# Layer 2's attention in a four-layer transformer kernel: the order of TensorE's work within a step

## The reference

```python
x = layernorm(...)                                   # [4, 256, 512]
q = rms_norm(x @ Wq + bq, gq)                        # [4, 256, 32 * 128]
k = rms_norm(x @ Wk + bk, gk)
v = x @ Wv + bv
# 32 heads of 128
p = softmax(q_h @ k_h.T / sqrt(128))                 # [4, 32, 256, 256]
o = p @ v_h
x = x + concat(o) @ Wo + bo
```

## Time and profile before

| | |
|---|---|
| median of 3 runs | 2597.18 us (2591.51 to 2602.34) |
| the profiled execution's own time | 2593.06 us |
| its span in the trace | 2591.2 us |
| granted TensorE clock, mean | 0.98 |
| busy: PE, DVE, ACT, POOL | 95%, 64%, 40%, 36% of the span |
| layer 2's attention stage | about 1488 to 2130 us of the span |

### The profile page before, as it was taken

How to read it: one execution, slowest core, us unless ns; L and a number is a source line. 1 busy time by engine, 2 the same in 40 slices (tenths; PEclk the granted TensorE clock), 3 DMA queues, 4 the chain that set the end, 5 groups by cost and what they waited for, 6 DMA issues and landing times. The chain is left out here.

```text
span 2591.2 us, 40725 instructions
## 1 busy us (share of the span) xinstructions
PE 2451.2 (95%) x14448; PEld 1958.6 (76%) x14448; DVE 1666.4 (64%) x2390; ACT 1030.5 (40%) x2030; POOL 941.3 (36%) x581
## 2 busy tenths in 40 slices
PE   5989999999969989999999989999999999999799
PEld 4767777678846668888888868888888887888566
DVE  5886557854487775544444457878777786543576
ACT  3322145433235533223333344555544543323453
POOL 3343210245230225124444455555455544430000
PEclk8999999999979999999999989999999999999899
DMA  2232264222342212234444422222222222331430
GB/s 86 61 111 74 62 109 86 33 40 44 50 98 54 39 31 40 45 102 146 146 145 143 139 71 90 90 89 81 68 80 79 73 43 38 54 47 31 98 66 34
DMA packets 404669, 195.31 MB, mean 75 GB/s; under 512 B 278856, under 2 KB 358192, under 8 KB 404542
## 3 DMA queue, kind: packets, MB, share of 16 engines
q1 hardware_dynamic: 404284, 193.10, 30.0%
q10 hardware_dynamic: 258, 0.49, 0.1%
HBM read 129.85 MB, written 44.04 MB: 67 GB/s over the span
## 5 line engine op out<-in xcount | busy, mean ns | idle before, releaser
L601 PE MATMUL banks<-xn_hi,w_hi 128*128 128x512 f32 x1264 | 495.9, 392 | 12.1 <-ACT sgf L1144 10.3
L601 PE MATMUL banks<-xn_hi,w_lo 128*128 128x512 f32 x1264 | 492.5, 390 | 0.0
L601 PE MATMUL banks<-xn_lo,w_hi 128*128 128x512 f32 x1264 | 492.4, 390 | 0.0
L601 PEld LDWEIGHTS banks<-xn_hi,w_hi 128*128 128x128 f32 x1264 | 237.7, 188 | 62.9 <-DVE w_lo L589 11.0
L601 PEld LDWEIGHTS banks<-xn_hi,w_lo 128*128 128x128 f32 x1264 | 237.5, 188 | 49.8
L601 PEld LDWEIGHTS banks<-xn_lo,w_hi 128*128 128x128 f32 x1264 | 237.7, 188 | 48.6
L3072 POOL TENSOR_TENSOR qk_raw<-qk_raw,rms 128x1024 f32<-128x1024 f32 x64 | 160.0, 2501 | 268.8 <-DMA qk_raw<-qk_scratch 257.2
L589 DVE TENSOR_TENSOR w_lo<-tw,w_hi 128x512 fp32r<-128x512 f32 (+2 forms) x136 | 117.6, 871 | 201.7 <-ACT w_hi L581 201.6
L2663 POOL TENSOR_TENSOR ssq<-ssq,sq 128x512 f32<-128x512 f32 x128 | 165.3, 1292 | 183.0 <-ACT sq L2634 183.0
L1256 POOL TENSOR_TENSOR h_lo<-sgf,h_hi 128x512 fp32r<-128x512 f32 (+1 forms) x94 | 127.8, 1363 | 282.6 <-ACT h_hi L1147 282.6
L2651 DVE TENSOR_SCALAR raw<-banks,cols 128x512 f32<-128x512 f32 x128 | 103.7, 810 | 180.3 <-ACT sq L2634 180.3
(11 more groups left out here) (299 smaller groups left out, 5833.6 us busy)
## 6 DMA issues: line engine op xcount, KB each, us to landing
qk_scratch<-raw SPq DMA_DIRECT2D x64, 512.0 KB, 3.0
qk_raw<-qk_scratch SPq DMA_DIRECT2D x64, 512.0 KB, 3.8
nat<-in_L_ffn_w SPq DMA_DIRECT2D x48, 256.0 KB
head_scratch<-stage SPq DMA_DIRECT2D x16, 512.0 KB, 3.2
st_qs<-st_hi SPq DMA_DIRECT2D x64, 128.0 KB, 2.6
nat<-in_L_attn_Wq SPq DMA_DIRECT2D x32, 256.0 KB
nat<-in_L_attn_Wk SPq DMA_DIRECT2D x32, 256.0 KB
nat<-in_L_attn_Wv SPq DMA_DIRECT2D x32, 256.0 KB
```

The costliest lines, as they stand in the source:

```text
L601: mm = nc.tensor.matmul(to[half][:, :], w[0:n, j, k * P:(k + 1) * P], r, start=first and k == 0 and x == 0, stop=last and k == len(rows) - ...
```

## The change

`outputs` of step n-1 is called directly ahead of `turns` of step n instead of at the step's end. Nothing else is edited, and the orders of VectorE, ScalarE, GpSimd and SP are the same row for row.

```diff
                     if real(8 * g + 4 + n // 2, s.v):
                         values(g, n)
+                    if real(i - 1, s.n):
+                        outputs(g + (n - 1) // GSTEPS, (n - 1) % GSTEPS)
                     if real(i, s.n):
                         turns(g, n)
                     if real(8 * g - 5 + n // 2, s.o) and not tail(g, n, 2):
                         project(g, n)
-                    if real(i - 1, s.n):
-                        outputs(g + (n - 1) // GSTEPS, (n - 1) % GSTEPS)
```

## The result

The change makes the kernel slower: 2606.45 us median of 10 runs (2599.43 to 2610.03) against 2595.85 (2591.51 to 2602.34), a ratio of 1.0038, interval 1.0027 to 1.0049. Run again it gives 2606.31 against 2597.65, 1.0035 [1.0022, 1.0049]. So it costs some 9 to 11 us (10.6 and 8.7 between the medians), where +2.0 was forecast: within 0.5%, with the sign forecast, and four to five times the size.

The account below looks back on a forecast made before the run. TensorE, busy 78.28 of 80 us, was taken as the bound, so only waits could move the time. Terms +2.5 - 0.3 - 0.2 = +2.0 us on a 2597.2 median gave 2599.2 us, range 2588 to 2610.

Parts of the forecast that it names:

- Steps without a wait: TensorE's step in layer 2's attention: its parts fill it without a gap, so it stays 4.78 us.
- The rival inside TensorE: New neighbours among TensorE's matmuls cost or save 0.05 us a step, 6.4 us either way; chance 0.08.
- (a): TensorE's products wait for VectorE's copied probabilities in the place where the turns did: the same wait, 0.
- (b): Products come 1.82 us earlier in their step, so ScalarE and GpSimd can start sooner; buys nothing directly: 0.
- (c): Turns come 0.86 us later, so VectorE's copy and, at step 7, the w_lo splits TensorE awaits slip; sum +2.0 us.
- The third group: At step 7, w_lo's first split falls 0.3 us behind GpSimd and loses the race: +2.5 us.
- The fourth and later groups: Waits for w_lo at step 7 shrink: -0.2 us in the fourth group, -0.1 in each of three later ones.
- both are inside GpSimd's instruction: Step 5, later groups: the output-weight split, ready at 1924.3 instead of 1923.7, still falls within GpSimd's instruction ending at 1925.9.
- the 1.18 us of cover: Step 7, later groups: VectorE already waits 1.18 us for ScalarE's w_hi, which covers the later copy.
- The start-up waits: TensorE's waits for GpSimd's low parts of queries and keys in the start-up have no reason to go.
- the shrinking stalls: Rival: GpSimd moves ahead, so step-5 VectorE gets in 1.4 us earlier; five groups save 1.3 each, -6.5 us; chance 0.16.
- The race lost everywhere: Rival: the slip changes which engine comes first at steps 5 to 8; five groups lose 2.5 each, +12.5 us; chance 0.14.

Follow-up runs that it names:

- experiment 3: The changed kernel with one of GpSimd's eight scalings of a group, the one meeting w_lo, cut from 1024 columns to 16: 2595.78 us, 0.9992.
- the first of experiment 4: The changed kernel with step 7 alone put back to the old order (turns, projection, products): 2604.54 us, 1.0026 against the unchanged kernel.
- experiment 2: Against the unchanged kernel, products moved between turns and projection: 2594.76 us, again 2594.97; or turns moved behind the projection, products last: 2607.53 us.
- the larger dose of experiment 2: The unchanged kernel with turns moved behind the projection, 1.39 us later, products still last: 2607.53 us, 1.0036.
- experiment 6: Two w_lo splits of step 7 ahead of VectorE's maximum, w_hi ahead of ScalarE's exponentials: 2603.61 us in the changed kernel, 2605.22 in the unchanged.

## Why the prediction was right, and where its size was off

**Steps without a wait: right.** 4.78 us as forecast, and the order with the turns left, which has other neighbours again, is no slower. The rival inside TensorE is out: experiment 3 has TensorE's order of after without its loss.

**(a) The copied probabilities: right** in after, where TensorE's list shows no such wait. In two other kernels with late turns (the first of experiment 4, and experiment 3) it appeared, 2.5 and 3.0 us in all.

**(b) The products earlier: right.** ScalarE's wait fell, GpSimd's wait for qk_hi fell from 23.4 to 16.3 us, and experiment 2 shows that it buys nothing.

**(c) The turns later: the place right, the sizes wrong.** Its chain (turns, copy, w_lo, TensorE) is what the experiments show: turns stay, no loss; turns 1.39 us later, a longer wait; the scaling cut short, no loss in the median. Three terms were off.

The third group was put at +2.5 us and was +0.5. The copy and w_lo came exactly where the prediction set them, 0.86 later and at once behind it. GpSimd did not stand still: it was expected 1.66 us before TensorE's moment as in the earlier trace rows, and started its scaling 1.21 before it. The wo_lo split of step 5, itself later, had stretched GpSimd's scaling there to 2.91 us from 2.48, which is most of the 0.45. So the race was won by 0.15 us instead of lost by 0.3.

The fourth and later groups were put at -0.2 and -0.1 and were +0.5, +0.8, +0.3 and +0.8. The step that failed reads "both are inside GpSimd's instruction": it held GpSimd's start fixed while VectorE's moved. In three of these four groups the order at step 5 turned round (wo_lo ahead of GpSimd by 0.07, 0.02 and 0.01 instead of 0.37, 0.24 and 0.27 behind), and with it VectorE's lateness, in the fifth and seventh the 1.18 us of cover, was gone. In the sixth the order and the cover stayed, and its wait is the +0.3. The prediction had named this as a sign of being wrong, later stalls that move by more than 0.5 us because GpSimd's phase has moved, and the sign came. With 0.8 in the second group the waits come to +3.7 instead of +2.0.

The clock had no term, and took 3.2 us. The start-up waits were put at nothing and grew by 0.8, and 0.8 more stays unplaced. Together +8.5 against +2.0, which is the mis-sized sum. That its sign is right is in part luck: the forecast had +2.5 from one lost race that was not lost, and -0.5 from the groups that in fact gave most of the growth.

Of the rivals, the shrinking stalls didn't come: experiment 2 has the early products of (b) without the late turns, and its gain is at most 0.2%. The race lost everywhere comes nearest in microseconds (+12.5 forecast) and has the wrong mechanism: the race was lost nowhere in after, it was won narrowly in four groups, and the second split pays in each.

**Open.** Why a median run of after lies 7 us above its profiled one: the second profiled execution shows 2.5 us of it in the stage. Which part of experiment 3 does it, the collision taken away or the phase moved. Why the larger dose of experiment 2 has longer waits and no larger median. Whether the 0.8 us of start-up waits belong to the change, and where the last 0.8 us go. And experiment 6's medians.

## What to carry to other kernels

When a queue of one engine shifts by less than a microsecond, the engine that takes turns with it at the memory, or feeds it, shifts too: work out both starts before deciding who wins a race, and look one loop earlier for who delays whom. A full engine pays for an order of work through the engines that serve it: put first in a step what the slower chain waits for, here the turns, whose copy leads to the next weights. And price a wait of a full TensorE by more than its length, since the clock may fall behind it.

## What the runs showed of the hardware

Two instructions in a row on VectorE and two on GpSimd take turns at the memory that both read: one GpSimd instruction let in between two splits makes 1.3 us into 3.46; one that is already running and a second in between make 5.26.

The granted clock fell to its lower level behind short waits of a TensorE that was otherwise full, once while the wait, of 4.03 us, still lasted. In the stage, over before, after and the kernels above, from the second group on 11 of 29 waits for w_lo of 1.80 to 4.03 us came with a spell at about 0.5, and none of those of 1.74 us or less. That is no general bound: past the stage, where TensorE is less full, the same wait of 1.16 us for VectorE's ln_sq was followed by such a spell in seven of the fourteen profiled executions, that of after among them, and not in that of before. In after a spell costs about 1.6 us. Why some waits are followed by one and others, as long, are not, the runs don't tell.
